# Routed slots of a two-layer kernel: rows turned by VectorE in 32x32 blocks instead of by TensorE

## What is computed

```
gate_logits = x @ gate_w.T + gate_b + expert_bias
top_idx = argmax(gate_logits)                      # one of 8 experts per row
for e in range(8):
    h = relu(x @ w1[e] + b1[e])                    # 256 -> 1024
    y = h @ w2[e] + b2[e]                          # 1024 -> 256
    out = out + (top_idx == e) * y
```

## Time and profile before

| | us |
|---|---|
| median of 3 runs | 1049.42 |
| lowest, highest | 1047.63, 1049.46 |
| span of the profiled execution | 1046.4 |

### The profile page before, as it was taken

How to read it: one execution, slowest core, us unless ns; L and a number is a source line. 1 busy time by engine, 2 the same in 40 slices (tenths; PEclk the granted TensorE clock), 3 DMA queues, 4 the chain that set the end, 5 groups by cost and what they waited for, 6 DMA issues and landing times. The chain is left out here.

```text
span 1046.4 us, 20027 instructions
## 1 busy us (share of the span) xinstructions
PE 1035.6 (99%) x6626; PEld 927.9 (89%) x6626; DVE 754.9 (72%) x1233; ACT 629.5 (60%) x1186; POOL 333.8 (32%) x291
## 2 busy tenths in 40 slices
PE   8999999999999999999999999999999999999998
PEld 7998888989889898898877888899999999888887
DVE  5875756656575566857779998876777777588887
ACT  4554445444444444545566666788888888566665
POOL 3353453444444344353452772000000000373000
PEclk9999999999999999999999999999999999999999
DMA  5216111010111201423156275588887876552203
GB/s 176 78 36 221 41 41 60 0 69 31 40 60 40 76 24 41 173 70 141 33 212 262 80 268 205 177 269 262 266 282 241 276 246 225 198 173 98 80 21 101
DMA packets 75139, 141.12 MB, mean 135 GB/s; under 512 B 9936, under 2 KB 43088, under 8 KB 74064
## 3 DMA queue, kind: packets, MB, share of 16 engines
q1 hardware_dynamic: 66320, 126.45, 35.5%
q0 software_dynamic: 3072, 8.39, 2.3%
q10 hardware_dynamic: 5696, 5.64, 1.6%
HBM read 101.86 MB, written 38.60 MB: 134 GB/s over the span
## 5 line engine op out<-in xcount | busy, mean ns | idle before, releaser
L775 POOL TENSOR_TENSOR acc<-acc,ytmp 128x512 f32<-128x512 f32 x120 | 156.5, 1304 | 248.2 <-ACT ytmp L870 227.1
L1572 ACT ACTIVATE act_o<-ps,scan_bias 128x512 f32<-128x512 f32 x189 | 129.7, 688 | 100.0 <-PE ps L388 95.8
L870 ACT ACTIVATE ytmp<-ps,sel 128x256 f32<-128x256 f32 x256 | 107.4, 471 | 99.8 <-PE ps L1104 99.1
L940 DVE SCALAR_TENSOR_TENSOR hT_l<-ps,hT_h 128x512 fp32r<-128x512 f32 x128 | 87.7, 685 | 104.8 <-ACT hT_h L829 104.6
L1102 PE MATMUL ps<-vals_h,hT_h 128*128 128x256 f32 x512 | 145.1, 283 | 0.8 <-DVE hT_l L940 0.7
L1103 PE MATMUL ps<-vals_l,hT_h 128*128 128x256 f32 x512 | 143.6, 280 | 0.0
L1104 PE MATMUL ps<-vals_h,hT_l 128*128 128x256 f32 x512 | 143.6, 280 | 0.0
L829 ACT ACTIVATE hT_h<-ps 128x512 fp32r<-128x512 f32 x128 | 76.3, 596 | 98.8 <-PE ps L388 98.6
L1724 POOL DMA_INDIRECT late_y<-y_d,pos_i x20 | 23.2, 1158 | 273.8 <-DMA y_d<-y_sb 268.0
L1896 DVE TENSOR_TENSOR_SCAN h_b<-a_b,hstate,xs_b 128x512 f32<-128x512 f32 x63 | 88.1, 1398 | 30.4 <-ACT a_b L1579 27.0
L386 PE MATMUL ps<-xT_h,keys_h 128*128 128x512 f32 x256 | 104.9, 410 | 1.2 <-DVE xT_l L427 1.2
(11 more groups left out here) (249 smaller groups left out, 2765.3 us busy)
## 6 DMA issues: line engine op xcount, KB each, us to landing
raw<-w SPq DMA_DIRECT2D x78, 512.0 KB, 5.3
x1T<-xT_d SPq DMA_DIRECT2D x16, 512.0 KB, 5.2
comb_b<-comb_d SPq DMA_DIRECT2D x8, 1024.0 KB, 7.4
w_small<-w SPq DMA_DIRECT2D x14, 512.0 KB, 5.0
xs_d<-zeros ACTq DMA_DIRECT2D x1, 4992.0 KB, 19.2
x_d<-x SPq DMA_DIRECT2D x8, 512.0 KB, 4.4
xn_d<-xn SPq DMA_DIRECT2D x8, 512.0 KB, 2.7
xT_d<-nT_h SPq DMA_DIRECT2D x8, 512.0 KB, 2.7
```

What stands on the lines that cost most here:

```text
L775: pool.tensor_tensor(dst[:, 2:4, :], acc[:, 2:4, :], ytmp[:, k % 2, :, :], ALU.add).then_inc(acc23, 1)
L870: act.activation(ytmp[:, k % 2, j - 2, :], yb(k, j), ACT.Copy, scale=sel[:, j, k:k + 1]).then_inc(y_23, 1)
L1572: act.activation(act_o[:, i % 2, w, :], ps[:, 3 * (i % 2) + w, :], func, bias=scan_bias[:, w, i:i + 1]).then_inc(act_g, 1)
```

## The change

`rows` has shape [128, 8, 64] instead of [128, 2, 256]. Four transfers load a slot's rows instead of one: transfer q writes partitions 32q to 32q+31 with columns 64q to 64q+63 of the rows, 32 rows per group (64 floats, 256 bytes, at a time instead of 1 KB). DVE then turns 32x32 blocks with one instruction (`turn_rows`) into `sT32`, a new SBUF tile, or for a small slot straight into `sT_small`. Feature 64q + 32c + a so lands on partition 32q + a of half c, and the host reorders w1's rows to match; the size and shape of w1's transfers are as before. TensorE's `rows_T` goes. ScalarE's copy to `sT_h` and DVE's subtraction for `sT_l` read `sT32`; ScalarE's copy for the small slot goes. The semaphore `turned` takes the place of `T_full`, for SP too; a big slot on TensorE waits for `sT_ok`, which now counts big slots alone, a small one for `turned`.

```diff
@@ buffers and views
-    rows = rc("rows", [P, ST, D], F32)
+    rows = rc("rows", [P, ST * P // Q32, DC * Q32], F32)
+    sT32 = rc("sT32", [P, DC, SLOT], F32)
-    xs_v = xs_d.rearrange("(b p) d -> b p d", p=P)
+    xs_q = xs_d.rearrange("(g r) (b k) -> b r g k", r=Q32, b=P // Q32)
@@ SP
             def load_rows(r, k):
                 n = ROUND * r + k
                 if not zero(n):
-                    wait_alone(sp, T_full, n)
+                    wait_alone(sp, turned, n)
                 b, st = blocks(r, k)
-                sp.dma_start(rows[:, 0:st, :], xs_v[bass.ds(b, st)].rearrange("b p d -> p b d")).then_inc(rows_in, 16)
+                n_q = P // Q32
+                for q in range(n_q):
+                    quarter = slice(q * Q32, (q + 1) * Q32)
+                    sp.dma_start(rows[quarter, 0:st * n_q, :],
+                                 xs_q[q][:, bass.ds(b * n_q, st * n_q), :]).then_inc(rows_in, 16)
@@ TensorE
-                    if i == MC - 3 and isinstance(g, int) and g == B_FIRST - 1:
-                        pe.wait_ge(fin_ok, g)
-                        rows_T(0, 0)
-            def rows_T(r, k):
...
-                for c in range(DC):
-                    for i in range(st):
-                        last_mm = pe.transpose(ps[:, 6, (c * st + i) * P:(c * st + i + 1) * P],
-                                               rows[:, i, c * P:(c + 1) * P], ident[:])
-                last_mm.then_inc(T_full, 1)
@@ in slot
-                pe.wait_ge(sT_ok, n + 1)
+                if small(k):
+                    pe.wait_ge(turned, n + 1)
+                else:
+                    pe.wait_ge(sT_ok, bigs(r, k) + 1)
...
-                if left(r, k) > 0:
-                    rows_T(r, k + 1)
@@ ScalarE
             def rows_hi(r, k):
...
+                act.wait_ge(turned, ROUND * r + k + 1)
+                act.activation(sT_h[:], sT32[:], ACT.Copy).then_inc(sT_hi, 1)
...
-                    rows_hi(r, k + 1)
+                    if not small(k + 1):
+                        rows_hi(r, k + 1)
@@ DVE
+            def turn_rows(r, k):
+
+                n, (_, st) = ROUND * r + k, blocks(r, k)
+                dve.wait_ge(rows_in, 16 * (P // Q32) * (n + 1))
+                dst = sT_small if small(k) else sT32
+                if not small(k) and not zero(n):
+                    dve.wait_ge(sT_ok, bigs(r, k))
+                dve.transpose(dst[:].rearrange("p c (g r) -> p g c r", r=Q32),
+                              rows[:, 0:st * P // Q32, :].rearrange("p g (c a) -> p g c a", c=DC)).then_inc(turned, 1)
+
             def rows_lo(r, k):
+                dve.wait_ge(turned, ROUND * r + k + 1)
                 dve.wait_ge(sT_hi, bigs(r, k) + 1)
-                dve.tensor_tensor(sT_l[:], ps[:, 6, :].rearrange("p (c t) -> p c t", c=DC), sT_h[:].bitcast(F32),
-                                  ALU.subtract).then_inc(sT_ok, 1)
+                dve.tensor_tensor(sT_l[:], sT32[:], sT_h[:].bitcast(F32), ALU.subtract).then_inc(sT_ok, 1)
@@ in slot, after w2_half(n, 1) and before the first low_e
+                if left(r, k) > 0:
+                    turn_rows(r, k + 1)
@@ in the scans of group 3, step MC - 4
+                    if g == B_FIRST - 1 and i == MC - 4:
+                        turn_rows(0, 0)
```

More of the change, by code:

```diff
@@ L51 @@
 CHUNK = 32
+Q32 = 32
 NL = M + E1
@@ L593, in build @@
     w1_hi, w1_lo, w2_hi, w2_lo = (sem(n) for n in ("w1_hi", "w1_lo", "w2_hi", "w2_lo"))
-    T_full, sT_hi, sT_ok = sem("T_full"), sem("sT_hi"), sem("sT_ok")
+    turned, sT_hi, sT_ok = sem("turned"), sem("sT_hi"), sem("sT_ok")
     l1_full, t_ok, e_hi, e_ok, l2_part, ys_ok, y_st = (
@@ L2068 @@
         "expert_bias": c(i["L1_ffn_expert_bias"]),
-        "w1": c(i["L1_ffn_w1"].reshape(E1, DC, P, 2, F1 // 2).transpose(0, 3, 2, 1, 4)),
+        "w1": c(i["L1_ffn_w1"].reshape(E1, P // Q32, DC, Q32, 2, F1 // 2).transpose(0, 4, 1, 3, 2, 5)
+                .reshape(E1, 2, P, DC, F1 // 2)),
         "b1": c(i["L1_ffn_b1"].reshape(E1, FJ, P).transpose(0, 2, 1)),
```

## The result

| | before | after |
|---|---|---|
| median of the runs of one set, us | 1048.53 (4 runs, 1047.46 to 1049.46) | 1055.32 (4 runs, 1054.25 to 1058.48) |
| span of the profiled execution, us | 1046.4 | 1056.7 |

The ratio is 1.0075, 95% interval 1.0063 to 1.0087: 0.75% slower, 6.8 us (0.65%) by the medians. The profiled execution of after is its slowest, 3.2 us above its median, so its span shows 10.3 us where the medians show 6.8. The first four experiments ran where the kernel before took 1047.09 us in the median. The later ones ran where even the kernel before spread from 1060 to 1088 us, with one run at 4955; for those I give the ratio of the two kernels' fast runs with its interval, and read the slot stage in the profile.

The account below looks back on a forecast made before the run. TensorE's 30.4 us round barely exceeds a loop through SyncE, which grows to 31.15 us and becomes the bound: +4.9 us by round 6, -0.9 after, +4.0 on the median 1049.42 gives 1053.4 us, range 1041 to 1061.

Parts of the forecast that it names:

- loop 31.15: Per-round cycle through SyncE's issues, landings and conversions: 29.8 - 0.3 + 1.65 = 31.15 us, longer than TensorE's new 29.3.
- A's list: SyncE's issues without a pause in a round's 256-row slot A, w2 load to w1 load: 9.1 us, forecast 10.7 or more.
- The price of an issue: Three more DMA issues per slot on SyncE at 0.55 us each: 1.65 us a round, bounds 1.5 and 2.5.
- rival 1: TensorE stays the bound, the issues cost nothing on SyncE's loop or landings shorten: faster, 1041.9 us; chance 0.19.
- 8.6 us off TensorE: 78 transposes at 0.11 us leave TensorE's path: 8.6 us in all, 1.1 a round, its round becomes 29.3 us.
- In B and S they are absorbed: Extra issues in a round's second 256-row slot and its 128-row slot vanish in SyncE's later waits for w1_lo and w2_lo.
- A alone: Four transfers only where SyncE issues in the first 256-row slot: loop 31.1 us, most of the loss stays, 1052 to 1054.
- Packets: Rows in 256 B packets at 17 ns: 0.5 us more a round in idle DMA time, cost taken as 0.
- rival 3: DMA engines become the bound if a 256 B packet costs what a 1 KB one does: 1071 us; chance 0.08.
- rival 4: DVE waits for rows or turns at 1.4 us, so eT_l comes late: up to 1.5 us a round, 1051; chance 0.08.
- The start: Round 0: three issues, 1.5 us, ahead of the w1 half delay its landing by 0.3 to 1.5 us, taken 1.0.
- Behind round 6: After the 128-row slot of round 6 starts, two groups of four transposes are still saved: -0.9 us.

Follow-up runs that it names:

- first four experiments: Changed kernel with rows by one transfer of 1 KB packets (1043.48 us), of 256 B (1045.18), four transfers only for small slots (1049.39), only for big slots (1046.89).

## Why the prediction was right, and where it wasn't

1. **The sign and the mechanism: right.** Forecast 1053.4 us, loop 31.15; measured 1055.32 and 31.7 (in the profile). The two kernels with four transfers and TensorE's transposes show it best: 1.0076 without any other part. The size was short: +4.0 us forecast, +6.8 by the medians. The listed signs are there in the main: A's list of 10.7 us and more, rounds of 31.7 in the mean (two of six just below 31), TensorE waiting for eT_l, ScalarE waiting for landings (24.7 + 7.6 us against 11.7 + 3.7). But the place is not the one named. TensorE waits 18 times, in slots of every kind and not once a round in B, and most of ScalarE's added wait is for w2; in B its wait for w1 is above 0.83 us in three of the six rounds.
2. **The price of an issue: right.** Three at 0.55 us on a list of 9.1 made 10.76; it is 10.7 to 11.2, against 9.0 to 9.2 in the kernel with one transfer. The rule of the Trainium skill, "DMA: Bandwidth & Descriptors", section "Issuing engines are not separate DMA queues", that the time to initiate a DMA is usually small relative to the DMA, would have made this rival 1 with 1041.9 us. It holds for these transfers by themselves (0.5 us against landings of 2 to 5), but not for what stands behind them in the list. The same section grants that issuing from several engines saves the sequencer's time. With GpSimd's queue A's list was 8.4 to 8.7 us, which agrees, but there the small packets went away too.
3. **"8.6 us off TensorE": over-sized.** One transfer gives 3.6 us in all, and rounds of 29.6, not 29.3: 0.76 us less than the usual 30.37 of before, not 1.1, and by S of round 0 it is 1.0 us late (687.89 against 686.87). The 0.11 us came from the chain, `L1491 x4` for 0.44. TensorE's timeline of before would have shown less: four transposes delay the next product by 0.36 us, and the two of slot B by 0.13 (711.23 to 711.36).

```profile
720.76 0.60 PE L1491 MATMUL ps<-ident,rows 128*128 128x128 f32 x4
721.12 0.36 PE L1532 MATMUL ps<-w_h,eT_h 128*128 128x256 f32 x1
```

   That makes 0.36 + 0.36 + 0.13 = 0.85 a round.
4. **"In B and S they are absorbed": wrong.** The later waits for w1_lo and w2_lo do take up SP's time, but four issues also stand ahead of loads that are needed, and b2b comes late for y_sb. Price 3.4 us with the packets of the big slots. In after the 512 KB loads of raw land in 5.9 us in the median from 690 to 870 us, against 5.3 before (the second and first line below), and those of b2b in 6.1 against 5.2.

```profile
raw<-w SPq DMA_DIRECT2D x59, 512.0 KB, 5.3
```

```profile
raw<-w SPq DMA_DIRECT2D x57, 512.0 KB, 5.9
```

   The forecast took landings as unchanged. With a landing of w1 and one of w2 on the loop this would be enough for the way from 31.15 to 31.7, but no run parts it from the rest. That those of raw lengthen only with all parts together (5.1 to 5.3 in the first four experiments) is measured; why isn't. Those of b2b take 6.2 us in the kernel with TensorE's transposes and four transfers as well, so for them the issues are enough.
5. **A alone: over-sized.** By the sum, four issues in A alone should give rounds of 31.15 too; they gave 30.5 in the mean, 29.6 to 31.8, so by the same sum the other parts of the loop were some 0.7 us shorter than in the turns that I had read. Points 4 and 5 cancel in part, which flatters the forecast.
6. **Packets: small, though twice the size.** Queue 1 is busy 36.1% of 1056.7 us against 35.5% of 1046.4: 10 us of all 16 engines. 19968 packets of 256 B replace 4992 of 1 KB (19.5 big slots' worth of rows), and the 69 further issues add 16 tiny ones each, which makes up the 21072 more under 512 B. With the bound of 54 ns for 1 KB and 5 for the tiny ones, one of 256 B takes at most about (160 + 270 - 6)/19.968 = 21 ns, an estimate, where I took 17, and a round 1.3 us more (10 over 7.8 rounds' worth), where I took 0.5. By time it is 1.7 us of the kernel. The 512 B of the Trainium skill, "DMA: Bandwidth & Descriptors", section "Specifications", are no cliff here: by this estimate a quarter of the bytes costs about 0.4 of the time, so the rate does fall, and rival 3 is refuted.
7. **The turn: right.** 0.7 us was taken for 128x512, and 705 ns is measured. The small one takes 437 ns.

```profile
L1942 DVE STREAM_TRANSPOSE sT<-rows x10: 701/705/711, 700.4 to 849.1; 128x512 f32<-128x512 f32 x10
L1942 DVE STREAM_TRANSPOSE sT_small<-rows x5: 436/437/438, 711.3 to 837.3; 128x256 f32<-128x256 f32 x5
```

   No DVE wait for rows stands in after's waits, so rival 4 fell, as the kernel with one transfer confirms.
8. **The start: right in size (1.4 us against 1.0), by luck.** The prediction put it down to the issues ahead of the w1 half's landing. The kernel with one transfer, without those issues, is 1.0 us late at the same point, so at most some 0.4 is theirs. In both TensorE's second layer of slot 0 starts 1.3 us later than before and runs at the lower clock. The transposes were cover there, not cost, and the prediction priced all 78 as cost.
9. **Behind round 6: wrong.** -0.9 us forecast, +1.6 in the profile of after, -0.6 in that of the kernel with one transfer. TensorE waits 2.5 us there in after (878 us to the end) and 0.8 before. SP issues no rows in the last two slots, so the four issues don't stand in their lists. What makes those waits longer no run looks at alone, and it stays open.

## What to carry to other kernels

When an engine's time is nearly matched by a loop through a queue, price the loop first: every DMA issue in an in-order list that never pauses is paid in full on each turn (0.5 to 0.55 us here), and cutting one transfer into four is no free change of layout. Ask where the new issues stand, and what lies behind them in the list; moving them to an idle queue (GpSimd here) gave most of the rounds back, moving them further down the same list only moved the wait to the consumer. Look at the packets on the page when a transfer changes its queue: they can change with it, and the experiment then tests two things. And work taken off the bounding engine where it happens to wait gives nothing, and may lengthen a pause.

## What the runs showed of the hardware

- Between the two layers of slot 0 TensorE paused for 2.63 us in eight profiles. In six of them its granted clock then went from 1.00 to the lower level for some 3 us, with 0.21 us from product to product instead of 0.12; in two it stayed at 1.00. Of two pauses of 2.04 us one did so. Those of 0.56 us and less left it at 1.00. For one kernel there is a profile of each kind: 7.34 us for the layer with the fall, 6.46 without.
- An fp32 multiplication of 128 columns by the identity ran as two instructions, 0.22 us each one (18 in 3.9 us), where a transpose on TensorE is one and delays the next product by 0.07 to 0.09 us.
- Transfers of rows cut into runs of 256 bytes went as packets of 256 B when SP issued them, and by the counts as 16 packets of 4 KB or 2 KB and 16 tiny ones per transfer when GpSimd did (17920 fewer packets under 512 B, 2688 more with 4.6 MB on queue 0).
- The transfers of rows are issued in 0.5 us each by SP and in 0.8 by GpSimd (0.58 busy and 0.22 between); they land in 3.4 to 3.8 us from GpSimd's queue, against 2.0 for the small and 5.0 for the big ones from SP's in after (medians, 690 to 870 us).
